# The last expert layer: fixed slot regions, routing merged with the layer ahead, and tiles that add into the output themselves

## What is computed

```python
# sublayer 7, end of _L3_xattn_ref: linear layers with ternary weights and globally quantised inputs
h = relu(bitnet_linear(concat(fused, avg_img), W_f1, b_f1))      # 512 -> 1024
x = x + bitnet_linear(h, W_f2, b_f2)                             # 1024 -> 256

# sublayer 8, _L3_ffn_ref, on xf = layernorm(x), T = 2048 tokens
logits = xf @ Wr + br                                            # 8 experts
top, idx = top_k(logits, 2); gates = softmax(top)
h = relu(xf @ W1[e] + b1[e])                                     # 256 -> 1024, fp32, chosen experts only
y = h @ W2[e] + b2[e]                                            # 1024 -> 256
x = x + sum over the two chosen experts of gate * y
```

## Time and profile before

| | us |
|---|---|
| median of 3 runs | 1935.74 (1931.85 to 1940.69) |
| profiled execution | 1932.1 |
| its span, first to last instruction | 1930.2 |
| mean granted TensorE clock | 0.880 |
| PE busy | 1474.6 (76%) |
| DVE busy | 1030.1 (53%) |
| ACT busy | 786.7 (41%) |
| POOL busy | 429.7 (22%) |

### The profile page before, as it was taken

The page is one execution under the profiler, slowest core; times in us unless marked ns, Lnnn a source line. Parts: engine busy times, 40 slices in busy tenths (PEclk is TensorE's granted clock), DMA queues, the critical chain, the costliest instruction groups (busy, mean ns, idle before and its releaser), DMA issues. The chain is left out here.

```text
span 1930.2 us, 28902 instructions
## 1 busy us (share of the span) xinstructions
PE 1474.6 (76%) x8619; PEld 1093.6 (57%) x8629; DVE 1030.1 (53%) x2339; ACT 786.7 (41%) x1810; POOL 429.7 (22%) x643
## 2 busy tenths in 40 slices
PE   2747999699999998465999877547554059999990
PEld 1546888577777776233777645315234036666660
DVE  2566888855555555686666555557671212222223
ACT  2323444465555553565655334356541012222220
POOL 0432223254433332001544200001000510000006
PEclk8767999899999999787999999669875579999995
DMA  9041000010000000000000000100009111111104
GB/s 340 31 142 32 23 22 22 3 44 2 1 1 1 2 1 1 33 0 3 1 1 1 1 22 1 47 1 0 1 4 345 66 66 33 33 33 33 33 28 130
DMA packets 54988, 76.34 MB, mean 40 GB/s; under 512 B 6377, under 2 KB 47089, under 8 KB 53873
## 3 DMA queue, kind: packets, MB, share of 16 engines
q1 hardware_dynamic: 51824, 66.80, 10.6%
q0 software_dynamic: 3072, 8.39, 1.3%
HBM read 55.00 MB, written 20.19 MB: 39 GB/s over the span
## 5 line engine op out<-in xcount | busy, mean ns | idle before, releaser
L1218 POOL TENSOR_SCALAR XT<-XT,l1x_rs 128x256 f32<-128x256 f32 x256 | 118.4, 483 | 189.5 <-DVE l1x_rs L1130 189.5
L1075 ACT ACTIVATE XT<-bank,l1x_nmax 128x256 f32<-128x256 f32 x256 | 118.9, 472 | 68.4 <-DVE l1x_nmax L1134 68.4
L1134 DVE TENSOR_REDUCE l1x_nmax<-bank 128x2 f32<-128x512 f32 x128 | 87.4, 684 | 109.3 <-PE bank L982 109.3
L2156 PE MATMUL bank<-l3f_wu,XT 128*128 x312 | 142.0, 598 | 0.7 <-ACT XT L2198 0.6
L2165 PE MATMUL bank<-l3f_wd,XT 128*128 x624 | 141.2, 379 | 1.6 <-DVE XT L2232 1.6
L994 PE MATMUL bank<-ident,XT 128*128 128x128 f32 x768 | 120.8, 280 | 9.0 <-POOL XT L1218 3.3
L2165 PEld LDWEIGHTS bank<-l3f_wd,XT 128*128 128x128 f32 x624 | 115.6, 190 | 16.4 <-issue 2.3
L790 DVE SCALAR_TENSOR_TENSOR X<-bank,l0f_gates,X 128x256 f32<-128x256 f32 x288 | 118.9, 475 | 0.3 <-PE bank L758 0.3
L994 PEld LDWEIGHTS bank<-ident,XT 128*128 128x128 f32 x768 | 84.4, 140 | 42.7 <-POOL XT L1218 24.4
L1141 DVE COPY l1x_pt<-bank 128x512 f32<-128x512 f32 x128 | 87.8, 686 | 30.5 <-PE bank L994 30.5
L2226 DVE COPY XT<-bank 128x512 f32<-128x512 f32 x39 | 27.0, 692 | 141.3 <-PE bank L2156 141.3
(11 more groups left out here) (494 smaller groups left out, 3811.5 us busy)
## 6 DMA issues: line engine op xcount, KB each, us to landing
l3f_wu<-in_L_ffn_W SPq DMA_DIRECT2D x8, 1024.0 KB, 13.8
l3f_wd<-in_L_ffn_W SPq DMA_DIRECT2D x8, 1024.0 KB, 12.1
slots<-zero SPq DMA_DIRECT2D x1, 4992.0 KB, 24.9
XT<-slots SPq DMA_DIRECT2D x39, 128.0 KB, 2.0
slot_out<-XT SPq DMA_DIRECT2D x39, 128.0 KB, 1.7
qweights<-tern_q SPq DMA_DIRECT2D x3, 1024.0 KB, 3.9
l0e_wu<-in_L_ffn_upT SPq DMA_DIRECT2D x18, 128.0 KB, 2.2
l0e_wd<-in_L_ffn_downT SPq DMA_DIRECT2D x18, 128.0 KB, 2.3
```

Source lines behind the costliest of these rows:

```text
L1075: act.activation(pr[n % 3][:, i, q, :], sc[(2 * n + i) % 3][:, q * S:(q + 1) * S], ACT.Exp, bias=nmax[:, n % 3, i, q:q + 1], accum_out=sum ...
L1134: dve.tensor_reduce(nmax[:, n % 3, i, :], sc[(2 * n + i) % 3][:].rearrange("p (q s) -> p q s", q=QT), AX, ALU.max, negate=True).then_inc(m ...
L1218: pool.tensor_scalar(t, t, rs[:, n % 3, i, q:q + 1], 1.0, ALU.mult, ALU.mult).then_inc(norm_ok, 1)
L2156: last = pe.matmul(up_b[half][:], xT[:, k, :], wu[:, ds(e * KD + k, 1), half * CH:(half + 1) * CH].rearrange("p a n -> p (a n)"), start=k ...
```

## The change

1. The two stages become one, *l3_both*. Its buffers are shared: the expert weights wu and wd have their place from the start of the stage, W1 of six experts is loaded right after the stage's layernorm, and the hidden layer lies inside the wd area. W2 is loaded chunk by chunk as the hidden layer is used up, W1 of the last two experts when the product with W_f2 is done.
2. *place_and_route* replaces the end block of l3_xattn, the layernorm, the router, place_tokens and the scatter block: one block, chunk by chunk. ACT scales and rounds to bf16 in one instruction (an offset of 128 does the rounding; a column sum takes it out again).
3. Each expert has a fixed region of 2048 slot rows, so a token's slot is known as soon as its chunk is counted, and its scatter can be issued at once. A row is 265 words wide: 256 features, the token's number and 8 gates. *tile_row* says where each of the 39 tiles starts.
4. 17,280 blank rows are written instead of 4992 zero rows, in nine DMAs, not at the start but in the block of the attention of sublayer 3 (*l1x*), behind the loads that SP issues there.
5. In *routed_tiles* each tile gathers its tokens' rows of the output from DRAM, adds gate * y, and scatters them back. X has been stored to the output before. Two tiles may hold the same token, so POOL gathers for tile i only when the scatter of tile i-1 has landed. `xs[u]` now also holds the indices and gates, and is loaded anew only when the tile's scatter has landed. The gather block at the end is gone, and so is slot_out.

```diff
 def start(K):
-            sp.wait_ge(zero_ok, 1)
-            sp.dma_start(K.slots.rearrange("(i p) d -> p i d", p=P),
-                         K.zero[:].unsqueeze(1).to_broadcast([P, SLOT_TILES, D])).then_inc(K.slots_zeroed, 16)
 cross_attention, SP:
                     load_attention_weights(K, sp, following)
+                    blank_slots(K, sp)
+EXPERT_ROWS = T
+SPARE_TILES = SLOT_TILES - T * TOP3 // P
+SLOT_ROWS = EXPERTS3 * EXPERT_ROWS + SPARE_TILES * P
+ROW = D + 1 + EXPERTS3
+ABSENT = 2 * T
+def blank_slots(K, sp):
+    tiles = SLOT_ROWS // P
+    step = 15
+    for at in range(0, tiles, step):
+        n = min(step, tiles - at)
+        sp.dma_start(K.slots[at * P:(at + n) * P, :].rearrange("(i p) d -> p i d", p=P),
+                     K.blank[:].unsqueeze(1).to_broadcast([P, n, ROW])).then_inc(K.slots_blank, 16)
+def place_and_route(...):
+  SP:
+                for c in range(NC):
+                    sp.wait_ge(q_ok, 2 * (c + 1))
+                    for e in range(2 * c, 2 * c + 2):
+                        sp.dma_start(K.wd[:, e * 8:(e + 1) * 8, :], a["L3_ffn_W2"][e]...).then_inc(K.w_loaded, 16)
+                sp.wait_ge(y_done, 2 * NC)
+                for e in range(E - 2, E):
+                    sp.dma_start(wu[:, e * KD:(e + 1) * KD, :], a["L3_ffn_W1"][e]...).then_inc(K.w_loaded, 16)
+                for c in range(NC):
+                    sp.wait_ge(x_ok, TPC * (c + 1))
+                    sp.dma_start(out[:, tiles, :], X[:, tiles, :]).then_inc(K.stored, 16)
+                sp.wait_ge(K.stored, 16 * NC)
+  ACT:
+                scale(0)
+                scale(1)
+                for c in range(NC):
+                    if c + 2 < NC:
+                        scale(c + 2)
+                    root(c)
+                    normalise(c)
+                    if c:
+                        exponentials(c - 1)
+                    copy_turned(c)
+                exponentials(NC - 1)
+  PE:
+                down(0)
+                down(1)
+                for c in range(NC):
+                    turn(c)
+                    logits(c)
+                    if c + 2 < NC:
+                        down(c + 2)
+                    count(c)
+  DVE:
+                add(0)
+                variance(0)
+                factors(0)
+                for c in range(NC):
+                    if c + 1 < NC:
+                        add(c + 1)
+                        variance(c + 1)
+                    shifted_logits(c)
+                    if c + 1 < NC:
+                        factors(c + 1)
+                    choose(c)
+                    place(c)
+                tables()
+  POOL:
+                for c in range(NC):
+                    xt = X[:, c * TPC:(c + 1) * TPC, :]
+                    pool.tensor_tensor(xt, xt, shift[:]..., ALU.add).then_inc(lifted, 1)
+                pool.wait_ge(K.slots_blank, K.slots_blank_n)
+                for c in range(NC):
+                    pool.wait_ge(slot_ok, 2 * (c + 1))
+                    for j in range(TPC):
+                        for i in range(k):
+                            pool.indirect_dma_start(K.slots, IndirectOffsetOnAxis(ap=slot[:, c, i, j:j + 1], axis=0),
+                                                    row[c * TPC + j], None).then_inc(scattered, 16)
+                pool.wait_ge(scattered, 16 * NT * k)
 def routed_tiles(...), SP:
-            def load(i, u):
-                sp.dma_start(xs[:, u, :], K.slots[ds(i * P, P), :]).then_inc(x_in[u], 16)
-            def store(i, u):
-                sp.wait_ge(y_ok, i + 1)
-                sp.dma_start(K.slot_out[ds(i * P, P), :], ys[:, u, :]).then_inc(y_out[u], 16)
+            def load(i, u):
+                first = sp.value_load(at(tile_row, i), min_val=0, max_val=SLOT_ROWS - P)
+                sp.dma_start(xs[:, u, :], K.slots[ds(first, P), :]).then_inc(x_in[u], 16)
             with sp.Fori(0, G - 1) as g:
                 for u in range(U):
-                    i = g * U + u
-                    sp.wait_ge(x_turned, i + 1)
-                    load(i + U, u)
-                    store(i, u)
+                    sp.wait_ge(y_out[u], 16 * (g + 1))
+                    load((g + 1) * U + u, u)
+  POOL:
+            for i in range(SLOT_TILES):
+                u, n = i % U, i // U + 1
+                index = bass.IndirectOffsetOnAxis(ap=xs[:, u, D:D + 1].bitcast(I32), axis=0)
+                if i:
+                    pool.wait_ge(y_out[(u - 1) % U], 16 * (n if u else n - 1))
+                pool.wait_ge(x_in[u], 16 * n)
+                pool.indirect_dma_start(acc[:, u, :], None, out, index, bounds_check=T - 1, oob_is_err=False).then_inc(acc_in[u], 16)
+                pool.wait_ge(y_ok, i + 1)
+                pool.indirect_dma_start(out, index, ys[:, u, :], None, bounds_check=T - 1, oob_is_err=False).then_inc(y_out[u], 16)
   DVE, output(i, u, n):
-                dve.tensor_tensor(ys[:, u, :], y_b[:, 0:D], b2[...], ALU.add).then_inc(y_ok, 1)
+                dve.tensor_tensor(ys[:, u, :], y_b[:, 0:D], b2[...], ALU.add).then_inc(y_biased, 1)
+                dve.wait_ge(y_biased, i + 1)
+                dve.wait_ge(acc_in[u], 16 * n)
+                dve.scalar_tensor_tensor(ys[:, u, :], ys[:, u, :], xs[:, u, ds(e + D + 1, 1)], acc[:, u, :], ALU.mult, ALU.add).then_inc(y_ok, 1)
 l3_both, a block after the layernorm:
+                for e in range(E - 2):
+                    sp.dma_start(wu[:, e * KD:(e + 1) * KD, :], a["L3_ffn_W1"][e]...).then_inc(K.w_loaded, 16)
+            POOL: memset ones, affine_select, memset lift, 8 x memset base, 2 x iota, tensor_copy
 l3_both, product with W_f1 (bit_linear written out, and ahead of it on PE):
+                for k in range(KN):
+                    last = pe.matmul(bank[7][:, 0:D], ones[:], q["f2"][:, k, :], start=k == 0, stop=k == KN - 1)
-def l3_ffn(K): ... layernorm, router, place_tokens, scatter block, gather block
```

More of the change, by code:

```diff
@@ new lines, in turn, with logits @@
+                def turn(c):
+                    pe.wait_ge(xn_ok, TPC * (c + 1))
+                    pe.wait_ge(xT_ok, KD * c) if c else None
+                    for kk in range(KD):
+                        for j in range(TPC):
+                            last = pe.transpose(turn_b[kk][:, j * P:(j + 1) * P], row[c * TPC + j][:, kk * P:(kk + 1) * P], K.ident[:])
+                        last.then_inc(t_done, 1)
+                def logits(c):
+                    pe.wait_ge(xT_ok, KD * (c + 1))
+                    if c:
+                        pe.wait_ge(lg_ok, c)
+                    for j in range(TPC):
+                        for kk in range(KD):
+                            last = pe.matmul(logit_b[:, j * E:(j + 1) * E], xT[c % 2][:, kk, j * P:(j + 1) * P], wr[:, kk, :], start=kk == 0, stop=kk == KD - 1)
+                    last.then_inc(logits_ok, 1)
@@ new lines, in count @@
+                def count(c):
+                    pe.wait_ge(chosen_ok, c + 1)
+                    if c:
+                        pe.wait_ge(pos_ok, c)
+                        pe.wait_ge(past_ok, c + 1)
+                    flat = chosen[:, c, :, :].rearrange("p t e -> p (t e)")
+                    pe.matmul(count_b[:, 0:TPC * E], const["before"], flat, start=True, stop=False)
+                    for u in range(1, TPC):
+                        last = pe.matmul(count_b[:, u * E:TPC * E], const["ones"], chosen[:, c, 0:TPC - u, :].rearrange("p t e -> p (t e)"),
+                                         start=False, stop=c == 0 and u == TPC - 1)
+                    if c:
+                        for u in range(TPC):
+                            last = pe.matmul(count_b[:, u * E:(u + 1) * E], const["ones"], past[:, c, :], start=False, stop=u == TPC - 1)
+                    last.then_inc(counted, 1)
@@ L2185, in body @@
                 turn_hidden(i)
-            for u in range(U):
-                body(u, u, 1, u == 0, False)
-            with pe.Fori(1, G - 1) as g:
-                for u in range(U):
-                    body(g * U + u, u, g + 1, False, False)
-            for u in range(U):
-                body((G - 1) * U + u, u, G, False, u == U - 1)
+            tiles(pe, body)
             down(SLOT_TILES - 1)
@@ new lines, in l3_both, with _ @@
+        global_quant(K, "l3q1", [([(VIS[:, k, :], qa[:, k, :]) for k in range(KD)], s[:, 2:3])], maxima=[vis_max[:]])
+        IMG = VIS
+        bit_linear(K, "l3l1", [(qa[:, 0:2, :], q["img"], D, IMG, s[:, 2:3], wsc["img"], bias["img"])], maxima=img_max)
+        with nc.Block() as block:
+            @block.vector
+            def _(dve):
+                for k in range(KD):
+                    K.dve_order.step(dve, dve.tensor_reduce(avg[:, k, :], IMG[:, k, :].rearrange("p (b s) -> p b s", s=S), AX, ALU.add))
+                dve.tensor_scalar(avg[:], avg[:], 1.0 / S, None, ALU.mult)
```

548 lines of the change are left out of this document (302 added, 246 removed).

## The result

The changed kernel takes 2032.96 us (median of four runs, 2030.5 to 2041.69) against 1935.13 (1931.85 to 1940.69): a ratio of 1.051, with a 95% interval of 1.049 to 1.054. It is slower by 5%, and the forecast was 1907. The profiled execution spans 2031.3 us against 1930.2, so 101.1 us are to be found.

| term | from, to | before | after | difference | forecast |
|---|---|---|---|---|---|
| 1 start | span's start to SP's first issue of l3_both | 1222.35 | 1208.82 | -13.5 | -12 |
| 2 front | to the RECIPROCAL of the last quantisation | 186.8 | 194.1 | +7.3 | +5 |
| 3 routing | to PE's first input transposes | 154.1 | 92.9 | -61.3 | -72 |
| 4 tiles | to the end of the last addition of b2 (DVE's L2221, now L2313) | 317.2 | 524.9 | +207.8 | +96 |
| 5 end | to the span's end | 49.7 | 10.6 | -39.1 | -46 |

What follows compares the result with a forecast made beforehand. PE bounds the tiles; around them, weight issue and engines working one at a time. Terms -12 + 5 - 72 + 96 - 46 = -29 from 1935.7 gave 1907 us, own range 1870 to 1945; the 0.8 range used bounds 1862 and 1952.

Steps and rivals of the forecast that it cites:

- term 4: Expert tiles: buffers freed only after the scatter lands make PE idle 2.65 us in each of 36 tiles, +96 us.
- the ring: Tiles: chain from input transposes through down, addition, scatter and load to the next transposes on that buffer, 10.6 us.
- clock still 1.0 there: Tiles: expected sign in the profile after, PE's granted clock staying at 1.0 despite about 2.7 us idle per tile.
- the first rival: Tiles: clock falls in the stalls; with half the tiles at 1.2 GHz, +192 for +96, time 2003; chance 0.08.
- Terms 1 and 2: Start: zero rows go, PE starts earlier, -12 us. Front of l3_both: new block and small work, +5 us.
- the blank rows: Sublayer 3: writing them takes an estimated 86 us, covered because no engine waits for a DMA there, so 0.
- Term 3: Last quantisation to first tile: routing with chunks overlapped takes 82 us in place of 154.1, -72 us.
- a sign of being wrong: Routing: the prediction would be wrong if POOL waits for slots between its chunks of scatters.
- the rival "in series": Routing: every chunk waits for the one before, 105 us instead of 75, time 1937, no change; chance 0.12.
- Term 5: End: 3.6 us behind the last addition in place of 49.7, -46 us.
- The second chain: Tiles: scatter of i-1, gather of i, addition take 6.4 us, inside the old 7.99 period, so no cost.

Runs made afterwards that it cites:

- e6_warmfull: Changed kernel with 30 dummy PE transposes per tile between the up matmuls and the wait for the next x: 1979.8 us.
- e2_warm: Changed kernel with 18 dummy PE transposes per tile between the up matmuls and the wait for the next x: 1978.2 us.
- e3_regfirst: Changed kernel with SP reading the tile's row number into its register ahead of the wait for the scatter, not behind it: 1978.2 us.
- e7_oldring2: Kernel before the change, with SP reloading a buffer only when its tile's store has landed, and that store made twice in series: 2081.7 us.
- e1_meta: Changed kernel with each tile's nine extra words loaded into their own area, so the next x load waits only for PE's input transposes: 1815.7 us.
- e11_lean: e9_meta2 without the 8 MB of W2 loads, and with the last tile's scatter replaced by a plain SP store into slots: 1815.0 us.
- e9_meta2: The kernel of e1_meta measured once more, unchanged, beside other runs on one chip: 1818.6 us.

## Why the prediction was wrong

**The step that failed is term 4**: the ring was right in its build and wrong in its size, and a falling clock was priced at nothing ("clock still 1.0 there"). Forecast: period 10.6, 36 x 2.65 = 96. Measured: 13.65 in the mean of those 36, and 504.1 - 298.9 = 205 us over the 38 periods. It has two parts, and e6_warmfull and e2_warm separate them.

*The ring is 12.1 us, not 10.6, at the full clock*: 36 x (12.1 - 7.98) = 148 in place of 96. By the rows of e6_warmfull, from the input transposes to DVE's TENSOR_TENSOR are 4.56 us, not 3.98 (1768.17 to 1772.73). The 3.98 came from the earlier trace rows, where PE doesn't stall; once it does, the start of the down group behind the input transposes is no longer hidden (0.32 "issue" here, 0.54 in the changed kernel). DVE's two instructions take 1.15 with their gaps, not 0.94. POOL wakes in 0.81, not 0.3: the 0.30 of the earlier trace rows is the gap between two POOL instructions that are both ready, and is no wake. Scatter to SP's issue was 3.3 in both, with the table read at 0.66 where the forecast had 0.7 (e3_regfirst).

*The clock falls in the stall*: 36 x (13.65 - 12.1) = 56. This was the first rival, at 0.08, with 2003 us. What I held against it, that the stall is shorter than the 4.92 us of the earlier trace rows and follows 8 us of dense work, proved nothing: the earlier trace rows showed that a stall of 4.92 suffices, and not that 2.7 doesn't. The rule of the Trainium skill that the prediction named beside that rival (TensorE: Matmul & The Clock Gate, Why this matters for your kernels) was the better guide: this trace agrees, with 5.30 us for L2265 behind 3.0 us of idle time. The runs go further: 2.0 to 2.5 us, a shorter gap than the page warns of, was enough for 18 of 39 groups in e7_oldring2. The rival's own argument was half right as well. The ring isn't hidden by the slower work, because only the matmuls right behind the stall are slow, 1.7 us per tile and not a whole tile's 8; and these lie inside the ring. At smaller stalls slow and quick tiles do mix, as it said, in e7_oldring2 one by one (also in e2_warm and e3_regfirst).

The two errors feed each other: by the table above, a stall of 2.2 to 2.4 us slows about half of the groups, and the ring that is 1.5 us longer than forecast brings it to 3.2 and nearly all of them. That is read from the table; no run has a ring of 10.6 to try it on.

**Terms 1 and 2** were right (-13.5 for -12, +7.3 for +5), the blank rows at nothing too.

**Term 3** was right in its build and 11 us too good in size. In e1_meta the first scatter starts 32.9 us in, the chunks follow in 10.4, 10.4 and 10.1, and the first tile stands at 81.6: forecast 32, 10.2 and 82. In the changed kernel's own profile it is 35.1, then 13.3, 10.9 and 15.9, and the tile at 92.9, through waits whose releaser the profile doesn't name. With them came a sign of being wrong that the prediction named, POOL waiting for slots between its chunks. Still the rival "in series" did not come about: the chunks overlap, POOL and DVE beside each other, and within a chunk POOL's scatters keep their gap of 0.30 us. What delays the engines there on one chip and not on the other stays open.

**Term 5**: -39.1 for -46. The gain is real, but 3.6 us behind the last addition of b2 was no possible end; it is 10.6. Left out were POOL's slow wake (0.5 more), the gather that the last addition has to wait for (0.47), and some 6.3 to 6.7 us between the landing of the last scatter and the span's end, for 0.4. Of these, 2.9 go with POOL's scatter in place of SP's store (e11_lean); what the rest is wasn't separated.

**The second chain** (scatter, gather, addition) was forecast at 6.4 and hidden. By the rows of e1_meta and e9_meta2 it is 2.9 to 3.3 from scatter to gather, 2.4 from there to the addition's start (1800.38 to 1802.74), and 1.3 to the next scatter: 6.6 to 7.0, hidden in 7.98 as it was meant to be.

The version that beats both kernels is e1_meta: 1815.7 and 1818.6 us in its two series, 6.2% below the kernel before. It keeps all of the change and frees x as early as before, by giving the nine words that live longer than x a place of their own.

## What to carry to other kernels

When a change lets one more reader use a buffer late, write out the ring anew, link by link, and take each link from a row in which that engine really was waiting: a gap between two ready instructions is no wake, and a latency from a stretch that never stalls leaves out what the stall uncovers. If the ring comes out longer than PE's own period, don't stop at the idle time, but price the matmuls behind it at the lower level of the clock as well. And if only a few columns of a buffer live long, load them apart.

## What was not expected of the hardware

- The clock's fall shows only in the matmuls behind the stall (16 of them in 5.3 to 5.4 us for 3.6 to 3.7, granted clock 0.50), and the up matmuls some 7 us later are at full speed again. Idle times with a median of 0.45 us per tile left the clock up, 1.2 gave 23% of slow tiles, 2.2 and 2.4 gave 46% and 59% in a regular pattern, 3.2 gave 92%.
- Filling the idle time with 3.4 us of useless transposes per tile made the tile stage 51 us shorter (503.8 to 452.8).
- POOL's indirect DMA starts 0.8 us behind the DVE instruction that releases it, at the last tile too (1.00 at 2022.46, addition ended at 2021.65), where DVE has nothing left to do; SP's store takes 0.03 there (e11_lean) and 0.19 in the earlier trace rows. So it isn't DVE's work beside it.
- A POOL scatter as the last work of the program took 3.7 us more to the span's end than a store by SP (9.7 and 6.0 us, e9_meta2 and e11_lean).
